# Three graph attention passes: gathering table rows edge by edge, or computing them densely from edge counts

## The reference, cut to what matters

```
xs = h @ Ws;  xd = h @ Wd                      # (3125, 4, 32)
alpha_s = sum(xs * a_s);  alpha_d = sum(xd * a_d)
e  = leaky_relu(alpha_s[src] + alpha_d[dst], 0.2)        # one logit per edge and head
ex = exp(e - max of e over the edges of dst)
out[n] = sum over edges with dst == n of xs[src] * ex / (sum of ex + eps) + bias
```

## Time and profile before

| what | value |
|---|---|
| median of 3 runs | 4972.12 us (4972.11 to 4972.57) |
| profiled execution: span, first to last instruction | 4975.7 us |
| time of the profiled execution beside its span | none listed; its span is 3.6 us above the median of the runs |
| DVE busy in the span | 3777.7 us (76%) |
| POOL busy | 2774.1 us (56%) |
| PE busy | 4016.0 us (81%), mean granted clock 0.906 |
| ACT busy | 2452.5 us (49%) |

### The profile page before, as it was taken

How to read it: one execution, slowest core, us unless ns; L and a number is a source line. 1 busy time by engine, 2 the same in 40 slices (tenths; PEclk the granted TensorE clock), 3 DMA queues, 4 the chain that set the end, 5 groups by cost and what they waited for, 6 DMA issues and landing times.

```text
span 4975.7 us, 70568 instructions
## 1 busy us (share of the span) xinstructions
PE 4016.0 (81%) x21002; PEld 2278.1 (46%) x21002; DVE 3777.7 (76%) x10209; ACT 2452.5 (49%) x5562; POOL 2774.1 (56%) x2853
## 2 busy tenths in 40 slices
PE   6999796888888568888865888888389999977799
PEld 3444344444444334444433444444267767644444
DVE  8999885898888769888885988888677777774211
ACT  5888703454454255545433554545366666663100
POOL 0000033777777677777767777777367777772000
PEclk9999897899998779999986999989699999987899
DMA  4444561344444334444432444444266777761566
GB/s 168 158 155 156 196 242 48 106 137 131 133 125 134 97 106 141 127 134 127 133 124 64 133 135 133 126 134 129 76 198 234 238 241 242 236 208 63 212 244 216
DMA packets 358410, 763.69 MB, mean 153 GB/s; under 512 B 73631, under 2 KB 274751, under 8 KB 357316
## 3 DMA queue, kind: packets, MB, share of 16 engines
q1 hardware_dynamic: 238396, 547.19, 29.9%
q0 software_dynamic: 89744, 193.14, 14.9%
q10 hardware_dynamic: 29944, 19.32, 1.5%
HBM read 392.63 MB, written 366.78 MB: 153 GB/s over the span
## 4 chain that ended last, share of the span: by engine, by line
POOL 30%; PE 16%; DVE 16%; issue 14%; DMA 7%; ACT 5%; POOLq 0%; SPq 0%; DVEq 0%; ACTq 0%
POOL big L776 28%; PE psT L1149 7%; DVE big L1911 3%; DMA big<-table,src_win 3%; DMA src_bc<-pe_src_d 2%; DVE big L1826 2%; DVE big L1925 2%; PE psT L1291 2%; PE psY L1291 1%; DVE big L1901 1%; PE psY L1405 1%; DVE big L1850 1%; PE psL L1291 1%; ACT hT L967 1%; POOL start_ad L744 1%
## 5 line engine op out<-in xcount | busy, mean ns | idle before, releaser
L776 POOL DMA_INDIRECT big<-table,src_win x2604 | 2512.3, 965 | 870.9 <-issue 760.9
L1911 DVE SCALAR_TENSOR_TENSOR big<-big,keep_win 128x132 f32<-128x132 f32 x2184 | 782.8, 358 | 77.8
L953 ACT ACTIVATE hT<-src_bc,node_c 128x640 bf16<-128x640 f16 x840 | 621.2, 814 | 146.9 <-PE psL L1291 83.8
L982 ACT ACTIVATE psH<-d_b 128x60 f32<-128x60 f32 x168 | 37.6, 224 | 1171.0 <-DVE d_b L1893 1171.0
L1291 PE MATMUL psT<-big 128*128 128x408 bf16 x1800 | 490.3, 338 | 55.0 <-DVE big L1826 55.0
L1291 PE MATMUL psT<-big,hT 128*128 128x408 bf16 x1200 | 374.8, 376 | 150.2 <-DVE big L1850 74.0
L1291 PE MATMUL psY<-big 128*128 128x408 bf16 x1800 | 490.0, 338 | 0.0
L958 ACT ACTIVATE hT<-hT 128x3200 bf16<-128x3200 bf16 x168 | 482.2, 2870 | 5.3
L1291 PE MATMUL psY<-big,hT 128*128 128x408 bf16 x1200 | 377.2, 379 | 103.6 <-DVE big L1850 67.8
L1826 DVE TENSOR_SCALAR big<-src_bc,node_c 128x640 bf16<-128x640 f16 x1260 | 407.5, 395 | 22.7 <-PE psL L1291 22.7
L728 POOL TENSOR_TENSOR dst_i<-big 128x512 f32<-128x512 f32 (+1 forms) x7 | 8.1, 1152 | 684.9 <-DMA big<-A_d 605.2
(11 more groups left out here) (372 smaller groups left out, 8323.4 us busy)
## 6 DMA issues: line engine op xcount, KB each, us to landing
rows<-big SPq DMA_DIRECT2D x168, 952.0 KB
big<-A_d SPq DMA_DIRECT2D x17, 6400.0 KB
rows<-big SPq DMA_DIRECT2D x112, 896.0 KB
A_d<-big SPq DMA_DIRECT2D x396, 200.0 KB, 1.9
big<-A_d SPq DMA_DIRECT2D x32, 1600.0 KB, 10.9
big<-table,src_win POOLq DMA_INDIRECT x2604
src_bc<-pe_src_d ACTq DMA_DIRECT2D x84, 128.0 KB
table<-big SPq DMA_DIRECT2D x15, 350.0 KB, 3.0
```

The lines of the kernel that those rows point to most:

```text
L776: pool.indirect_dma_start(out=rows[:, k, 0:p.table_w], out_offset=None, in_=table, in_offset=bass.IndirectOffsetOnAxis(ap=src_win[:, s, k: ...
L953: ins = nc.scalar.activation(hot_of[t], src_bc[:, q % 2, :], ACT.Square, bias=node_c[:, t:t + 1], scale=-1.0)
L1911: v.scalar_tensor_tensor(state[:, k, 0:GATW], prev[k][:, 0:GATW], kw[:, 0, k:k + 1], rows[:, k, 0:GATW], ALU.mult, ALU.add).then_inc(chain ...
```

## The change

The table, the gathers, the one-hots and the lane walk go from the three GAT layers. Instead, each layer multiplies over all source and destination nodes with the counts as weights:

- Destinations are taken in 8 chunks of 400 (`CH`), sources in 25 tiles of 128, heads in 4. For each chunk, tile and head, DVE *bends* the logits into the leaky relu (`bend`: row plus per-partition scalar, maximum with a second row, 128x400), ACT takes the exponential into PSUM, DVE *weighs* it with the counts (`weigh`: minimum with a cap, times counts, 128x400), and PE multiplies it by that head's 32 features and a one (33 columns, float32) and adds up in PSUM, two heads in one bank at partitions 0 and 64. Three buffers (`MOVING`) of bent logits rotate.
- The destination's largest logit is bounded for each chunk: PE multiplies 25 tiles of bf16 level marks with the high halves of the counts (`levels`), DVE reads the exponent out of the sum (`highest`), PE and DVE turn it into rows (`top_rows`, `near`), which PE spreads over partitions (`spread_row`, `keep_rows`) and ACT copies (`near_row`). For a next chunk of the same layer `levels` stands after source tile 17 on PE, `highest` after tile 17 on DVE, `near` after tile 18; for the first chunk they stand before tile 0.
- After a chunk, ACT and DVE copy the sums out (`move_sums`, `ev`), PE spreads numerators and denominators (`shares`), DVE divides (`divide`, after tile 3 of the next chunk), ACT adds the bias (`layer_rows`).
- Before each layer `settle` finds the range of the source terms and fills the level marks (3,200 elements a partition).
- SP loads the counts again in halves of a chunk (13 and 12 source tiles) into a ring of three, 24 chunks in all. POOL has no work in the three layers. The buffers move to fit.
- After the last layer PE transposes back to rows (25 tiles), DVE adds to `xt` and takes the moments. Parts that only the GAT lanes needed go from the set-up (`fresh`, `start_i`, `dfirst_i`, the zeroed `start_ad`), `keep` is made after the GAT layers. PNA and the dense layers keep their work, with constants written out.

The core of the diff (indentation shortened):

```diff
+    for J in range(NH):
+        a = CHB * (J % NCH)
+        for late in range(2):
+            k = 2 * J + late
+            if k >= RING:
+                sp.wait_ge(ring_used, k - RING + 1)
+            q = (NT - SPLIT) * W if late else HALF_W
+            sp.dma_start(a_half[k % RING][:, :, 0:q], A_d[a:a + CHB, :, HALF_W * late:HALF_W * late + q].rearrange("b p q -> p b q")
+                         ).then_inc(a_part[k % RING], 16)
...
-                rows = gathered_rows(p, s)
-                for k in range(p.dma_steps(s)):
-                    pool.indirect_dma_start(
-                        out=rows[:, k, 0:p.table_w], out_offset=None, in_=table,
-                        in_offset=bass.IndirectOffsetOnAxis(ap=src_win[:, s, k:k + 1], axis=0)
-                    ).then_inc(gathered[s], 16)
...
+            for t in range(NT):
+                n = NT * J + t
+                for h in range(H):
+                    k = H * n + h
+                    act.wait_ge(bent_v, H * n + h + 1)
+                    if k >= 2:
+                        act.wait_ge(weight_rdy, k - 1)
+                    nc.scalar.activation(psE[k % 2], soft[n % MOVING][h], ACT.Exp,
+                                         bias=s_all[:, 2, t, h:h + 1]).then_inc(soft_rdy, 1)
+                if c and t == 4:
+                    layer_rows(g, J - 1)
+                if c < NCH - 1 and 20 <= t < 20 + H:
+                    near_row(J + 1, t - 20)
+            move_sums(J)
+        layer_rows(g, NCH * g + NCH - 1)
...
+        nc.tensor.matmul(psS[0:H, 0:CH], w_att[:, g, D + H:D + 2 * H], feat[g % 2][:, CH * (J % NCH):CH * (J % NCH + 1)],
+                         start=True, stop=True)
+        for t in range(NT):
+            ins = nc.tensor.matmul(psH[:, 0:CH].rearrange("l (b w) -> l b w", w=W), lev[:, t, :, :].rearrange("p h k -> p (h k)"),
+                                   marks_of(J, t), start=(t == 0), stop=(t == NT - 1))
+        ins.then_inc(lev_ps, 1)
...
+    def keep_rows(J):
+        for h in range(2):
+            if J:
+                pe.wait_ge(bent_v, H * NT * J - 1 + h)
+            nc.tensor.matmul(psV[h], to_all[:, 2 + h, :], v_4, start=True, stop=True).then_inc(near_ps, 1)
+    def shares(J):
+        pe.wait_ge(ev_rdy, 4 * (J + 1))
+        for a in range(2):
+            nc.tensor.matmul(psS[:, 0:CH], spread[0:64 + HC, a, :], ev[0:64 + HC, a, :], start=(a == 0), stop=(a == 1))
+        for a in range(2):
+            ins = nc.tensor.matmul(psH[:, 0:CH], spread[0:64 + HC, 2 + a, :], ev[0:64 + HC, a, :], start=(a == 0), stop=(a == 1))
+        ins.then_inc(share_ps, 1)
...
+            for t in range(NT):
+                n = NT * J + t
+                if t == 0 and J:
+                    pe.wait_ge(ev_rdy, 4 * J)
+                if t == 23 and c < NCH - 1:
+                    keep_rows(J + 1)
+                for a in range(2):
+                    pe.wait_ge(weight_rdy, H * n + 2 * a + 2)
+                    for k in range(2):
+                        ins = nc.tensor.matmul(acc[a][64 * k:64 * k + HC, 0:CH], xs_1[:, t, 2 * a + k, :], soft[n % MOVING][2 * a + k],
+                                                   start=(t == 0), stop=(t == NT - 1))
+                ins.then_inc(summed, 1)
+                if c and t == 2:
+                    shares(J - 1)
+                if c < NCH - 1:
+                    if t == 17:
+                        levels(g, J + 1)
+                    if t == 18:
+                        top_rows(J + 1)
+                    if 19 <= t < 19 + H:
+                        spread_row(J + 1, t - 19)
+        shares(NCH * g + NCH - 1)
...
-                v.tensor_tensor(for_heads, for_heads, over_heads(by_edge(cw_p[:, :, 1:15]), HC), ALU.mult).then_inc(chained, 1)
...
-                for k in range(1, p.steps):
-                    after(8 + k)
-                    v.scalar_tensor_tensor(state[:, k, 0:GATW], prev[k][:, 0:GATW], kw[:, 0, k:k + 1],
-                                           rows[:, k, 0:GATW], ALU.mult, ALU.add
-                                           ).then_inc(chained if k < p.steps - 1 else updated, 1)
...
+    def highest(J):
+        dve.wait_ge(lev_ps, 2 * J + 1)
+        link(v.tensor_single_scalar(bits.bitcast(I32), psH[:, 0:CH].bitcast(I32), 23, op=ALU.arith_shift_right))
+        v.tensor_scalar(bits, bits.bitcast(I32), float(LOW + STEEP), float(LOW), ALU.min, ALU.max).then_inc(near_rdy, 1)
+    def near(J):
+        dve.wait_ge(lev_ps, 2 * J + 2)
+        link(v.tensor_scalar(m_4, psH[0:H, 0:CH], ends_4[:, 3:4], ends_4[:, 5:6], ALU.mult, ALU.add))
+        link(v.tensor_tensor(v_4, m_4, psS[0:H, 0:CH], ALU.add))
+        link(v.tensor_scalar(v_4, v_4, 0.0, DEEPEST, ALU.max, ALU.min))
+        v.tensor_tensor(v_4, v_4, m_4, ALU.subtract).then_inc(near_rdy, 1)
+    def bend(n, h):
+        J, t = n // NT, n % NT
+        if t == 0:
+            dve.wait_ge(row_rdy, H * J + 1 + h)
+            if h >= 2:
+                dve.wait_ge(near_ps, 2 * J + h - 1)
+        if n >= MOVING:
+            dve.wait_ge(summed, n - MOVING + 1)
+        row = row_v[J % 2][:, 4 + h, :] if h < 2 else psV[h - 2]
+        v.scalar_tensor_tensor(soft[n % MOVING][h], row, s_all[:, 1, t, h:h + 1], row_v[J % 2][:, h, :],
+                               ALU.add, ALU.max).then_inc(bent_v, 1)
+    def weigh(n, h):
+        J, t = n // NT, n % NT
+        k = H * n + h
+        dve.wait_ge(soft_rdy, k + 1)
+        v.scalar_tensor_tensor(soft[n % MOVING][h].rearrange("p (b w) -> p b w", w=W),
+                               psE[k % 2].rearrange("p (b w) -> p b w", w=W), CAP, counts_of(J, t),
+                               ALU.min, ALU.mult).then_inc(weight_rdy, 1)
+    def tile_weights(n, bends):
+        J, t = n // NT, n % NT
+        if t == 0 or t == SPLIT:
+            k = 2 * J + (t == SPLIT)
+            dve.wait_ge(a_part[k % RING], 16 * (k // RING + 2))
+        for h in range(H):
+            weigh(n, h)
+            if bends:
+                bend(n + 1, h)
+        if t == SPLIT - 1 or t == NT - 1:
+            dve.wait_ge(weight_rdy, H * n + H)
+            dve.sem_inc(ring_used, 1)
+    def divide(J):
+        dve.wait_ge(share_ps, J + 1)
+        if J:
+            dve.wait_ge(out_rdy, J)
+        link(v.tensor_scalar(share, psH[:, 0:CH], GAT_EPS, None, ALU.add))
+        link(v.reciprocal(share, share))
+        v.tensor_tensor(share, share, psS[:, 0:CH], ALU.mult).then_inc(share_rdy, 1)
...
+    for g in range(3):
+        settle(g)
+        for c in range(NCH):
+            J = NCH * g + c
+            if c == 0:
+                highest(J)
+                near(J)
+                for h in range(H):
+                    bend(NT * J, h)
+            for t in range(NT):
+                n = NT * J + t
+                tile_weights(n, t < NT - 1 or c < NCH - 1)
+                if c and t == 3:
+                    divide(J - 1)
+                if c < NCH - 1:
+                    if t == 17:
+                        highest(J + 1)
+                    if t == 18:
+                        near(J + 1)
+            dve.wait_ge(summed, NT * (J + 1))
+            if J:
+                dve.wait_ge(share_ps, J)
+            for at in (0, 64):
+                v.tensor_copy(ev[at:at + HC, 1, :], psZ[at:at + HC, 0:CH]).then_inc(ev_rdy, 1)
+        divide(NCH * g + NCH - 1)
```

More of the change, by code:

```diff
@@ new lines, in gather @@
+                    for k in range(p.dma_steps(s)):
+                        pool.indirect_dma_start(
+                            out=rows[:, k, 0:p.table_w], out_offset=None, in_=table_d,
+                            in_offset=bass.IndirectOffsetOnAxis(ap=src_win[:, s, k:k + 1], axis=0)
+                        ).then_inc(gathered[s], 16)
+            gather(0)
+            with pool.Fori(1, p.rounds, 1) as rnd:
+                gather(rnd)
+            for r in range(ROWS_SLOTS):
+                pool.wait_ge(rows_out[r], p.groups // ROWS_SLOTS * 16)
@@ L1112, in _ @@
+            nc.scalar.activation(bn[:, 2, :], bn[:, 1, :], ACT.Sqrt, bias=eps[:, 0:1]).then_inc(bn_std, 1)
+            for b in range(NB + 1):
+                if b < NB:
+                    deviation(3, b)
+                if b:
+                    normal(3, b - 1)
+            keep_hT(3)
             for b in range(NBK + 2):
```

1570 lines of the change are left out of this document (682 added, 888 removed).

## The result

The changed kernel takes 5357.8 us (median of 4 runs, 5354.6 to 5372.0) against 4972.3: a ratio of 1.0782, 95% interval 1.0767 to 1.0798. Forecast were 5257 us, the range 5140 to 5420. So it is slower as forecast, by 385 us where 285 were worked out. It lies in the range, but 18 us above the sum's own case (5180 to 5340), in the part that the range held for rival A.

The account below looks back on a forecast made before the run. GpSimd's gathers were taken to pace the old GAT passes, VectorE the new. Terms 2455 + 231 + 88 + 92 + 152 + 28 = 3046 us against 2761, +285, gave 5257 us, range 5140 to 5420.

Parts of the forecast that it names:

- the sum's own case: Whole kernel: the summed terms hold, within 0.03 us a unit and a third on the waits; 5180 to 5340 us, chance 0.66.
- rival A: New layers: TensorE's clock drops to half level, lengthening `levels` and chunk ends; +130 us, 5390 us, chance 0.13.
- the gathers' 805 us a pass: Old GAT passes: 644 gathers at 1.25 us on GpSimd take 805 of the 826 us window.
- 0.54 + 0.48 us a unit: Steady tiles: VectorE's `bend` and `weigh` make a unit of 1.02 us; 600 tiles take 2455 us.
- The reciprocal: Division, 24 times: 400 elements at 6.25 ns each take 2.65 us of the division's 3.85.
- The drains of the old program order: Once a chunk: next chunk's rows 11.0 us (231 in all), chunk end 3.65 (88), division 3.85 (92).
- `shares` on PE (2.7) fits under tile 3: Before each division: TensorE's 2.7 us of `shares` is covered by tile 3, so VectorE has no wait, 0 us.
- A projection at a layer's start: Start of each layer: 25 projections at about 0.5 us with ACT's copy, 13.5 us.
- the wait in `highest`: After tile 17, 21 times: VectorE idles 6.1 us while TensorE finishes the tile and runs `levels`.
- B: Steady tiles: TensorE binds at the half clock without overlap, 5.4 us a tile, about 6020 us; chance 0.04.
- C: Steady tiles: idle GpSimd makes VectorE's operations cheaper, at the bare 0.42 us, 4820 us; chance 0.07.
- D: Drains: half of the waits are hidden while VectorE's own work stays, 5140 us; chance 0.07.

Follow-up runs that it names:

- relu: `bend` as one tensor_scalar from SBUF in all heads, without the second row and `keep_rows`, against the changed kernel: 4837.4 us, ratio 0.9711.
- the three moves: Division behind tile 5, sum copies in the next chunk's first tile, `levels` spread over earlier tiles, together against the changed kernel: 5148.6 us, ratio 1.0336.
- filler2: Four zero-weight bf16 matmuls added behind each pair of heads of tiles 0 to 23, against the changed kernel: 5352.4 us, ratio 1.0749.
- busy_pool: GpSimd given three unread 128x384 additions per source tile in the three layers, against the changed kernel: 5595.6 us, ratio 1.1245.
- filler: Three unread bf16 matmuls added on TensorE behind each of tiles 5 to 15 of every chunk, against the changed kernel: 5397.8 us, ratio 1.0852.

## Why the prediction was right, and where it was short

**Right.** That the gathers' 805 us a pass would be replaced by VectorE's pace, at 0.54 + 0.48 us a unit: 2455 forecast, 2459 measured. That the 0.48 of `weigh` held to the second digit is in part luck, since it came from the row of another operation, a reduction. `relu` shows by experiment that the pace is VectorE's, since the unit fell by what VectorE's instruction fell (0.21 us). The choice to go by the rows, too, against the table of the Trainium skill, VectorE: DVE Perf Modes, section on the TRN2 errata, by which, an estimate, a unit would have been 1.05 us: `bend` has one spacing, 0.54, with its row in PSUM and in SBUF, and `weigh`, which reads PSUM, is shorter. The reciprocal was 2.65 us as worked out from the two shorter ones. The drains of the old program order were there, once a chunk and in their places, and the three moves took them away one by one. PNA and SAGE stayed.

**Short by 100 us, for the most part at one step.** The sum had the drains at TensorE's full clock and kept the low clock as rival A, with a chance of 0.13. Its condition came true: 0.62 over the layers, under the 0.7 that I had named. So the likeliest case should have been the sum with A's drains. `filler2` shows 60 us of the shortfall to be the clock's; up to 97 are, if the cheapest drains are what the full level gives everywhere. The row for it was in hand: an engine with heads side by side would be busy 35 to 40% of a tile, and at 37 and 43% the clock had been 0.64. I set it against "no matmul of the trace is that narrow". The records show that the pairs do run side by side: at the full level the second pair of a tile starts 0.70 us behind the first (2194.75 and 2195.45 us above), where I had 0.67 for a single head.

**A's own price was in the wrong place.** It put 5 us a chunk on `levels` and 1 on the chunk's end, 130 us. The clock rises during these 25 matmuls (0.50 before most of them, 0.78 to 0.88 over the drain), so a chunk lost 1.3 us there in the mean (8.0 for 6.7), 0.7 at each chunk end, 0.8 at `near`, and 1.8 in front of the division, which the sum had called covered: "`shares` on PE (2.7) fits under tile 3". It does at the full level. At the half it takes 5.5 us behind a TensorE that is already late, and the division waits 2.4 where it did. That was the one wait that neither the sum nor A had.

**Smaller.** A projection at a layer's start takes 0.86 us and not 0.5: 25 took 21.5 us in the second and third layer, and 27.3 in the first, where other transposes stand among them, for 12.5. Shorter terms beside it made most of that good. The terms that the sum lists for the wait in `highest` (1.3, 0.67 and 4.3, less 0.5) give 5.8 us and not its 6.1, some 7 us in 21 chunks. The units' own small waits made 21 us where I had none.

**The rivals.** B (TensorE binds, 5.4 us a tile) did not occur. C fell as a forecast, because nothing came cheaper than the row of a quiet stretch; `busy_pool` shows that its premise is worth 230 us when GpSimd adds beside VectorE; what the gathers on GpSimd cost VectorE in the kernel before, no run shows. D fell: the waits stood in program order, and only moving them hid them.

## What to carry to other kernels

Cost a wait for TensorE at the clock that TensorE will have where the wait is, and read that from a stretch like the one just before it; a mean over the stage does not tell it. Work that comes once in a block and drains the pipeline was cheaper here to spread or to put a tile or two later (222 us) than to speed up (16 us). And before moving part of an elementwise load to an idle GpSimd, look whether VectorE's instructions beside it read two SBUF tensors, or are of the kind that took 0.33 us here alone and 0.54 beside it: rewriting the instruction so that VectorE needs one tensor was worth 530 us here, and the helper 13.

## What was not expected of the hardware

- GpSimd beside VectorE: a two-tensor SBUF operation went from 0.62 to 0.99 us, a tensor_scalar from a spacing of 0.33 to 0.54, operations with a tensor in PSUM stayed at 0.56 and 0.62.
- The granted clock does not follow the busy share: 0.50 at 77% busy (22.97 of 30 us), and 1.00 in `filler` at 53% (5.31 of 10). At the half level the same matmuls look busier.
- The clock moved inside single drains. Five of the 21 `highest` in the changed kernel were entered at 1.00; in two it stayed there (6.8 us each), in three it fell inside (8.3 us). In `filler2` all ran at 1.00 (7.0 us), and in 15 of 21 chunks the clock then fell behind `levels`, where TensorE waited for VectorE (2.6 us, up to 1343.94, in the chunk of the windows above).
